# The opening of a graph network and Performer kernel rebuilt: one set of statistics for two normalisations

## What is computed

```python
def _layernorm(x, axis=-1, eps=1e-05):
    m = jnp.mean(x, axis=axis, keepdims=True)
    v = jnp.var(x, axis=axis, keepdims=True)
    return (x - m) / jnp.sqrt(v + eps)
...
    xn = _layernorm(x, axis=-1)
    x = x + _L0_gnn_ref(xn, edge_index, ...) + _L0_mix_ref(xn[None], ...)[0]
    x = x + _L0_ffn_ref(_layernorm(x, axis=-1)[None], ...)[0]
    return x
...
            for l in range(depth):
                h = _layernorm(x, ln1_s[l], ln1_b[l])
                q = heads(h @ Wq[l] + bq[l])
                k = heads(h @ Wk[l] + bk[l])
                v = heads(h @ Wv[l] + bv[l])
                qp = _softmax_kernel(q, proj[l], True)
                kp = _softmax_kernel(k, proj[l], False)
                attn = _linear_attention(qp, kp, v)
                x = x + (attn @ Wo[l] + bo[l])
```

## Time and profile before

| what | us |
|---|---|
| median of 3 runs | 1339.37 |
| lowest and highest of them | 1329.63, 1345.73 |
| profiled execution, its own time | 1338.45 |
| its span (first to last instruction) | 1336.6 |
| TensorE busy in it | 1186.8 (89%) |
| VectorE busy | 847.0 (63%) |
| ScalarE busy | 311.2 (23%) |
| GpSimd busy | 316.4 (24%) |

### The profile page before, as it was taken

How to read it: one execution, slowest core, us unless ns; L and a number is a source line. 1 busy time by engine, 2 the same in 40 slices (tenths; PEclk the granted TensorE clock), 3 DMA queues, 4 the chain that set the end, 5 groups by cost and what they waited for, 6 DMA issues and landing times.

```text
span 1336.6 us, 16673 instructions
## 1 busy us (share of the span) xinstructions
PE 1186.8 (89%) x5940; PEld 936.6 (70%) x5960; DVE 847.0 (63%) x1727; ACT 311.2 (23%) x584; POOL 316.4 (24%) x223
## 2 busy tenths in 40 slices
PE   1699979999999989887999999997888899899695
PEld 0577879888788877677998878884434588687432
DVE  7767447769953366764777995335787415616766
ACT  2234334423111003443442311100111112011212
POOL 4420200104733313020010563240000143300306
PEclk9899789999999989998999999999999999899897
DMA  6400100101312110000010131142000010101001
GB/s 197 157 1 1 32 1 1 32 1 48 111 32 64 36 56 1 0 31 2 1 33 1 53 105 42 54 185 78 1 1 0 9 32 32 32 1 30 1 0 63
DMA packets 15786, 52.12 MB, mean 39 GB/s; under 512 B 2624, under 2 KB 3456, under 8 KB 15200
## 3 DMA queue, kind: packets, MB, share of 16 engines
q1 hardware_dynamic: 11488, 39.18, 9.0%
q10 hardware_dynamic: 4224, 11.91, 2.5%
HBM read 44.80 MB, written 6.29 MB: 38 GB/s over the span
## 4 chain that ended last, share of the span: by engine, by line
PE 55%; DVE 23%; issue 15%; ACT 4%; POOL 2%; DMA 1%; SPq 0%; POOLq 0%; DVEq 0%; ACTq 0%
PE ps_a L401 6%; PE ps_v L401 6%; PE ps_a L403 6%; PE ps_a L402 6%; PE ps_v L402 6%; PE ps_v L403 6%; PE ps_v L556 5%; PE ps_a L658 4%; DVE f_hi L1157 4%; PE ps_v L762 2%; PE ps_v L569 2%; DVE f_lo L1159 2%; DVE expk L1269 2%; DVE ht_lo L1159 2%; PE ps_a L422 2%
## 5 line engine op out<-in xcount | busy, mean ns | idle before, releaser
L401 PE MATMUL ps_a<-ht_hi,w_hi 128*128 128x512 f32 x496 | 195.1, 393 | 2.4 <-DVE most_i L1429 2.4
L402 PE MATMUL ps_a<-ht_lo,w_hi 128*128 128x512 f32 x496 | 193.7, 391 | 0.0
L403 PE MATMUL ps_a<-ht_hi,w_lo 128*128 128x512 f32 x496 | 193.6, 390 | 0.0
L978 POOL TENSOR_TENSOR w_lo<-stage,w_hi 128x1024 fp32r<-128x1024 f32 x58 | 148.8, 2566 | 32.8 <-issue 28.5
L786 ACT ACTIVATE work<-ps_a,col_sb 128x512 f32<-128x512 f32 x96 | 66.4, 719 | 331.4 <-PE ps_a L403 207.7
L976 POOL CAST w_hi<-stage 128x1024 fp32r<-128x1024 f32 x58 | 67.9, 1171 | 242.4 <-PE ps_a L403 138.5
L1343 DVE TENSOR_TENSOR xm<-ps_v,xm 128x512 f32<-128x512 f32 x80 | 55.2, 690 | 94.4 <-PE ps_v L403 94.0
L401 PE MATMUL ps_v<-w_hi,ht_hi 128*128 128x512 f32 x224 | 94.5, 422 | 21.6 <-issue 8.8
L401 PEld LDWEIGHTS ps_a<-ht_hi,w_hi 128*128 128x128 f32 x496 | 93.5, 189 | 24.4 <-issue 2.6
L403 PEld LDWEIGHTS ps_a<-ht_hi,w_lo 128*128 128x128 f32 x496 | 93.5, 189 | 19.9
L402 PEld LDWEIGHTS ps_a<-ht_lo,w_hi 128*128 128x128 f32 x496 | 93.6, 189 | 19.5
(11 more groups left out here) (190 smaller groups left out, 2208.0 us busy)
## 6 DMA issues: line engine op xcount, KB each, us to landing
stage<-wstream SPq DMA_DIRECT2D x62, 512.0 KB, 3.6
nat<-x ACTq DMA_DIRECT2D x8, 256.0 KB, 6.4
xt_d<-xt_hi SPq DMA_DIRECT2D x1, 2048.0 KB, 6.3
xt_d<-xt_lo SPq DMA_DIRECT2D x1, 2048.0 KB, 10.8
ht_hi<-xt_d ACTq DMA_DIRECT2D x1, 2048.0 KB, 9.6
ht_lo<-xt_d ACTq DMA_DIRECT2D x1, 2048.0 KB, 15.4
x_again<-x ACTq DMA_DIRECT2D x8, 256.0 KB, 4.2
out<-xm SPq DMA_DIRECT2D x8, 256.0 KB, 2.0
```

The costliest lines, as they stand in the source:

```text
L401: nc.tensor.matmul(ps, left[0], right[0], start=first, stop=False)
L402: nc.tensor.matmul(ps, left[0], right[1], start=False, stop=False)
L403: return nc.tensor.matmul(ps, left[1], right[0], start=False, stop=last)
L978: nc.gpsimd.tensor_tensor(lo, stage[:, j, :], hi.bitcast(f32), ALU.subtract).then_inc(w_split, 1)
```

## The change

1. VectorE takes one set of statistics of x, by halves, and GpSimd makes both inverse deviations from it: `rstd` for the layer's normalisation (`first_deviation`) and `rstd_x`, `shift_x` for the residual.
2. x is loaded over two queues, even tiles on ScalarE's, odd ones on SyncE's, with a semaphore for each half; the identity goes in between, the edge ends and small constants behind the first weights.
3. VectorE normalises straight into `nat1`, half 0 before the statistics of half 1; ScalarE writes the residual `xm` later, after the first half's copies.
4. The first weights in the stream are V's. Their high part is made by ScalarE and their low part by VectorE. K's follow (ScalarE and GpSimd), then Q's (GpSimd).
5. The transposes of the residual and their split stand between V's tiles (after the fifth and the seventh), and x transposed is stored in three pieces from other places (`xt_hi` in slot 3, `xt_lo` in `nat`).
6. The block numbers, their maximum and the rounding of the head mask stand on VectorE behind V's last tile. TensorE waits for the mask ahead of K's product instead of at its start.
7. The output bias is added to the residual in attention's first eight `at` steps, in both layers, no longer behind each tile of V.
8. GpSimd's program is now: deviations, K's low weights (once half 0 of the input is split), Q's weights (once half 1 is), maximum over the partitions, bounds, and then the sums of V.

```diff
-HELPED = 2
+HELPED = 1
...
+XT_ORDER = [("xt", h, k) for h in range(H) for k in range(KT)]
+LATER_A = (
+    QK_ORDER
     + [("ddq", g, j) for g in range(STEPS) for j in range(2)]
     + [("o", h, k) for h in range(H) for k in range(KT)]
     + F0_ORDER
     + [block for c in range(1, FC) for block in by_halves(("f", c))]
 )
+
+A_JOBS = [numbered(N1_ORDER + (XT_ORDER if L == 0 else []) + LATER_A) for L in range(LAYERS)]
+A_OFF = [0, len(A_JOBS[0])]
...
-MIX_W = numbered(["q", "v", "k", "o"] + FFN_ORDER)
+W_NAMES = ["v", "k", "q", "o"] + FFN_ORDER
+MIX_W = numbered(["v", "k", "q", "o"] + FFN_ORDER)
+SLOT_OF = {"q": 0, "v": 1, "k": 2, "o": 3} | {name: n % SLOTS for n, name in enumerate(FFN_ORDER)}
...
+            for t in range(1, NT, 2):
+                sp.dma_start(nat[:, t, :], x[t * P:(t + 1) * P, :]).then_inc(x_in[t // 4], 16)
+                if t == 3:
+                    sp.dma_start(ident[:], ident_c).then_inc(ident_in, 16)
+            for j in range(PIECES):
+                sp.dma_start(stage[:, j, :], wstream[0, j]).then_inc(w_in[j], 16)
...
-            sp.wait_ge(a_empty, done(XT - 1))
-            for i in range(2):
-                sp.dma_start(xt_d[i], xt[i][:].bitcast(f32)).then_inc(xt_stored, 16)
+            sp.wait_ge(a_empty, done(A_JOBS[0][XT_ORDER[-1]]))
+            for n in range(2):
+                sp.dma_start(xt_d[0, :, 2 * n:2 * n + 2, :], xt_hi[n][:].bitcast(f32)).then_inc(xt_stored, 16)
+            sp.dma_start(xt_d[1], xt_lo[:].bitcast(f32)).then_inc(xt_stored, 16)
...
-            pe.wait_ge(consts_in, 96)
-
-            pe.wait_ge(mask_ready, 1)
-
-            for n in range(XT):
-                h, k = divmod(n, KT)
-                if k == 0:
-                    pe.wait_ge(x_normed, 4 * (h + 1))
-                turn(bank_a(n), [Xm[:, 4 * h + i, nodes(k)] for i in range(4)], a_full)
+            pe.wait_ge(ident_in, 16)
...
+                def turn_residual(h):
+                    pe.wait_ge(x_normed, 4 * (h + 1))
+                    for k in range(KT):
+                        turn(bank("a", ("xt", h, k)), [Xm[:, 4 * h + i, nodes(k)] for i in range(4)], a_full)
...
+                    if L == 0 and t in (4, 6):
+                        turn_residual(t // 2 - 2)
+                if L == 0:
+                    pe.wait_ge(mask_ready, 1)
...
-            for t in range(NT):
-                act.dma_start(nat[:, t, :], x[t * P:(t + 1) * P, :]).then_inc(x_in, 16)
+            for t in range(0, NT, 2):
+                act.dma_start(nat[:, t, :], x[t * P:(t + 1) * P, :]).then_inc(x_in[t // 4], 16)
+            act.dma_start(col_sb[:], cols[0]).then_inc(par_in, 16)
...
+            high_weight(0, SLOT_OF["v"])
+            load_parameters(0)
...
+                    if L == 0 and name == N1_ORDER[KT - 1]:
+                        high_weight(1, SLOT_OF["k"])
+                        act.wait_ge(rstd_x_ready, 1)
+                        for t in range(NT):
+                            nc.scalar.activation(Xm[:, t, :], nat[:, t, :], ACT.Identity, scale=rstd_x[:, t:t + 1],
+                                                 bias=shift_x[:, t:t + 1]).then_inc(x_normed, 1)
+                if L == 0:
+                    for name in XT_ORDER:
+                        _, h, k = name
+                        act.wait_ge(a_full, a0 + (MIX_A[name] + 1))
+                        nc.scalar.activation(xt_hi[k // 2][:, k % 2, half(h)], psA[:, MIX_A[name] % BANKS, :],
+                                             ACT.Copy).then_inc(xt_high, 1)
...
-            low_weight(0, 0)
-            both_halves(0, 0)
-            for s in range(1, HELPED):
-                low_weight(s, s)
-            both_halves(0, LN_FIRST)
+            def first_deviation(h):
+                columns = slice(4 * h, 4 * h + 4)
+                pool.wait_ge(var_ready, h + 1)
+                hold(pool)
+                nc.gpsimd.tensor_scalar(vare[:, columns], mv[:, columns, 1], 1.0 + EPS_LN, EPS_LN * EPS_LN, ALU.mult,
+                                        ALU.add).then_inc(eps_added, 1)
+                pool.wait_ge(eps_added, h + 1)
+                nc.gpsimd.tensor_tensor(rstd[:, columns], vare[:, columns], nhalf[:, columns], ALU.pow).then_inc(rstd_ready, 1)
+
+            first_deviation(0)
+            first_deviation(1)
+            nc.gpsimd.tensor_scalar(rstd_x[:], mv[:, 0:NT, 1], EPS_LN, None, ALU.add).then_inc(p_chain, 1)
+            pool.wait_ge(p_chain, 2)
+            nc.gpsimd.tensor_tensor(rstd_x[:], rstd_x[:], nhalf[:, 0:NT], ALU.pow).then_inc(p_chain, 1)
+            pool.wait_ge(p_chain, 3)
+            nc.gpsimd.tensor_tensor(shift_x[:], mv[:, 0:NT, 0], rstd_x[:], ALU.mult).then_inc(p_chain, 1)
+            pool.wait_ge(p_chain, 4)
+            nc.gpsimd.tensor_scalar(shift_x[:], shift_x[:], -1.0, None, ALU.mult).then_inc(rstd_x_ready, 1)
+            pool.wait_ge(split, done(MIX_SPLIT[N1_ORDER[KT - 1]]))
+            low_weight(1, SLOT_OF["k"])
+            pool.wait_ge(split, done(MIX_SPLIT[N1_ORDER[-1]]))
+            split_weight(2, SLOT_OF["q"])
...
-            pool.wait_ge(xt_stored, 32)
-            split_weight(2, 2)
+            pool.wait_ge(xt_stored, 48)
+
+            LATE_USERS = [(5, 6, 4), (4, 5, 6)]
...
-                for n in range(8, 15):
-                    kind, c = FFN_ORDER[n - 8]
+                for n, (kind, c) in zip(range(8, 15), [FFN_ORDER[i] for i in (0, 1, 2, 3, *LATE_USERS[L])]):
...
-            dve.wait_ge(ends_in, 32)
-            then(nc.vector.tensor_scalar(block_i[:], ends_i[:, 1, :], 7, None, ALU.arith_shift_right))
-            then(nc.vector.tensor_copy(block_f[:], block_i[:]))
-            for r in range(2):
+            def block_spans(r):
                 for b in range(NT):
                     last = nc.vector.scalar_tensor_tensor(out=spans[:, r, b, :], in0=block_f[:], scalar=float(b),
                                                           in1=group_no[:, r, :], op0=ALU.is_equal, op1=ALU.mult)
-            then(last)
-            nc.vector.tensor_reduce(span_p[:], spans[:], axis=AX.X, op=ALU.max).then_inc(span_ready, 1)
-            dve.wait_ge(consts_in, 96)
-            nc.vector.tensor_copy(headmask_r[:], headmask[:]).then_inc(mask_ready, 1)
-
-            dve.wait_ge(x_in, 16 * NT)
+                return last
+
             residual = lambda t: Xm[:, t, :]
-            normalise(lambda t: nat[:, t, :], Xm, x_normed)
-
-            dve.wait_ge(x_normed, NT)
-            deviations(residual, 0, LN_FIRST)
-
-            def split_input(h):
-                for k in range(KT):
-                    n = h * KT + k
-                    dve.wait_ge(xt_high, n + 1)
-                    nc.vector.tensor_tensor(xt[1][:, k, half(h)], psA[:, n % BANKS, :],
-                                            xt[0][:, k, half(h)].bitcast(f32), ALU.subtract).then_inc(a_empty, 1)
-
-            split_input(0)
-            normalise_half(residual, nat1, normed, 0, 0, LN_FIRST)
-            split_input(1)
+            loaded = lambda t: nat[:, t, :]
+
+            def low_weight(s, slot):
+
+                for j in range(PIECES):
+                    whole = slice(2 * j, 2 * j + 2)
+                    hi, lo = (w[:, slot, whole, :].rearrange("p a b -> p (a b)") for w in (Whi, Wlo))
+                    dve.wait_ge(w_high, s * PIECES + (j + 1))
+                    nc.vector.tensor_tensor(lo, stage[:, j, :], hi.bitcast(f32), ALU.subtract).then_inc(w_split, 1)
+
+            for h in range(H):
+                dve.wait_ge(x_in[h], 64)
+                statistics(loaded, half_tiles(h))
+                aggregate(half_tiles(h), h + 1)
+                if h == 0:
+                    normalise_half(loaded, nat1, normed, 0)
+            low_weight(0, SLOT_OF["v"])
...
+                def split_residual(h):
+                    for k in range(KT):
+                        dve.wait_ge(xt_high, h * KT + k + 1)
+                        nc.vector.tensor_tensor(xt_lo[:, k, half(h)], psA[:, MIX_A[("xt", h, k)] % BANKS, :],
+                                                xt_hi[k // 2][:, k % 2, half(h)].bitcast(f32), ALU.subtract).then_inc(a_empty, 1)
...
-                    nc.vector.tensor_tensor(Xm[:, t, :], Xm[:, t, :], rows_sb[:, 2, :], ALU.add)
                     if t == 2:
                         for k in range(KT):
                             split_t(("n1", 1, k), hT, k, 1)
+                    if L == 0 and t in (4, 6):
+                        split_residual(t // 2 - 2)
+                if L == 0:
+                    dve.wait_ge(ends_in, 32)
+                    then(nc.vector.tensor_scalar(block_i[:], ends_i[:, 1, :], 7, None, ALU.arith_shift_right))
+                    then(nc.vector.tensor_copy(block_f[:], block_i[:]))
+                    block_spans(0)
+                    then(block_spans(1))
+                    nc.vector.tensor_reduce(span_p[:], spans[:], axis=AX.X, op=ALU.max).then_inc(span_ready, 1)
+                    dve.wait_ge(consts_in, 80)
```

(5 more changed lines are left out.)

76 lines of the change are left out of this document (32 added, 44 removed).

## The result

| | before | after |
|---|---|---|
| median of the runs | 1342.02 us (4 runs, 1329.63 to 1345.73) | 1364.74 us (4 runs, 1357.32 to 1369.73) |
| ratio, 95% interval | | 1.0181 (1.0098 to 1.0264) |
| profiled execution, span | 1336.6 us | 1367.9 us |
| mean granted clock of TensorE, in shares of 2.4 GHz | 0.957 | 0.924 |
| the same kernels once more (run e14 below) | 1342.88 us (29 runs) | 1353.14 us (12 runs: eleven from 1335.19 to 1378.92, one of 1578.61) |

The forecast was 1336.0 us, range 1323 to 1344: wrong. The kernel became slower, by 1.8% in the first set of runs and by about 0.8% at the medians of the second (ratio 1.0054, interval 1.0011 to 1.0097).

A forecast was written before the change was run, and what follows sets the result against it. VectorE's chain in the opening, ahead of V's product, was taken to bound the kernel. 7.3 us gained, less 2.5 for sums and 3.0 for adds, plus 0.7, took 2.5 us off 1338.45: 1336.0 us, range 1323 to 1344.

The forecast's parts named there:

- x at 6.0 us: Opening: the first half of x, four loads over two queues, has landed at 6.0 us (bounds 4.4 and 8.4).
- Inverse deviation 1.4: Opening: the step from the variances to VectorE's first normalisation takes 1.4 us, besides any library load.
- V's low weights 2.8: Opening: VectorE makes V's low weights, two of 128x1024, in 2.8 us ahead of the splits.
- GpSimd's library, 7.3 us: Opening: GpSimd's code load, now behind the wait for the first variances, delays the normalisation 7.3 us (bounds 0 and 13.5).
- Rival B: Opening: GpSimd's library costs nothing at the start, 7.3 us better, 1328.7 us; chance 0.2.
- The mask's wait, 7.1 us: Ahead of K's product: TensorE waits for V's copy, 0.7 us, and the block work, 6.4 us.
- The slow clock behind it, 2.0 us: Behind the wait for the mask: TensorE's slow clock costs 2.0 us, leaving 7.3 us of the gain.
- The sums beside K's product, 2.5 us: K's product: GpSimd's seven sums of V now run beside it and cost 2.5 us (bounds 0 and 10.3).
- K's product by 66 to 76 us: Sign: K's product starts near 71 us; before 66 or after 76 us the prediction is wrong in the main.
- The adds in attention, 3.0 us: Attention, both layers: 16 output-bias adds of 0.68 us cost 3.0 us, about 1.5 a layer (bounds 0 and 10.9).
- Rival D: Attention is bound by VectorE, so the adds cost 10.9 instead of 3.0 us, 1343.9 us; chance 0.12.
- Rival E: K's product: the port lock makes GpSimd's sums cost 10.3 instead of 2.5 us, 1343.8 us; chance 0.08.

The follow-up runs named there:

- e14: The changed kernel once more, unedited, on another chip than its first runs: 1353.14 us.
- e7: The changed kernel with two adds ahead of each context-product wait, block numbers made between V's tiles and the head mask copied behind V's fourth: 1316.24 us, ratio 0.9830.
- e8: e7 with GpSimd's seven sums of V put ahead of the span and the bounds in layer 0: 1321.35 us, ratio 0.9838.

## Why the prediction was wrong

By its own steps:

- x at 6.0 us: 5.78. Statistics 3.0: 3.0. Inverse deviation 1.4: 1.9 from the aggregation's end to the normalisation. V's low weights 2.8: 2.3. Splits 4.3: 4.4. Right.
- GpSimd's library, 7.3 us: nothing. Its first arithmetic came 0.5 us behind the variances (8.78 to 9.31). Rival B. The rows 6.03 and 7.30 of the earlier trace rows stand beside library changes in the middle of the program, and no row showed one at the start; I gave the likelier place to the nearest row, where the bound of 0 was the case. At the change of library after the span, 9.93 us of "issue" stand again. The Trainium skill's 6 us for freshly loaded code (GPSIMD Engine Reference, "Instruction dispatch") does not show at the start.
- The mask's wait, 7.1 us: 7.2. The slow clock behind it, 2.0 us: K's product to the first square took 4.7 us against 3.0. Right, and by e7 worth undoing.
- The sums beside K's product, 2.5 us: the stage grew by 3.8 us (60.5 to 64.3). VectorE's part is in the groups of that stage, the changed kernel's first, with the mean ns of one behind the comma, then those of before:

```profile
L1280 DVE TENSOR_TENSOR sq_lo<-sq,sq_hi 128x512 fp32r<-128x512 f32 x15 | 12.4, 825 | 0.5
...
L1278 DVE CAST sq_hi<-sq 128x512 fp32r<-128x512 f32 x15 | 7.0, 464 | 14.3 <-ACT sq L871 14.2
```

```profile
L1237 DVE TENSOR_TENSOR sq_lo<-sq,sq_hi 128x512 fp32r<-128x512 f32 x15 | 10.4, 692 | 0.5
L1235 DVE CAST sq_hi<-sq 128x512 fp32r<-128x512 f32 x15 | 6.4, 426 | 10.1 <-ACT sq L846 10.0
```

That is 15 x 0.17 = 2.6 us. e8 takes 3 us back. Right in size.
- K's product by 66 to 76 us, else wrong in the main: it was at 59.9, 11.2 us early. 7.7 of them are the start of V's product, with the library. The rest is V's product itself, which ran 14.7 us from its fifth tile to its end where the forecast had 16.7: it carried over the 2.0 us of slow clock of the earlier trace rows, but with the wait of 6.2 us shrunk to 1.2 us the clock was full there (1.00 from 26.0 to 52.7 us). The opening with K's and Q's product gained 14.9 us where the sum had 4.8, and this unforeseen gain hid a part of the loss in attention.
- **The adds in attention, 3.0 us: this is the step that failed.** It priced an add by its own length and TensorE's wait by its own length, and put the clock at nothing. In its own terms it was of the right size: TensorE's idle time grew by 2.5 us in layer 0 and 2.7 us in layer 1, and taking from every profiled stage half of its slow stretches leaves 119.4 us on average for the 12 stages without an add in the steps and 121.6 us for the eight with all of them, a collision and no filling, so some 2 us a layer. What the sum lacked was the clock: 51 us of the changed kernel's attention in layer 0 and 68 us in layer 1 ran at 1.2 GHz, against 29 and 10 before, which costs half of the difference, 11 and 29 us of the 13.8 and 29.3. Not all of it is the collision's: in each layer 12 us are the stretch behind the eighth add, and in layer 1 another 7 are the one in the third context product and 10 the one at the stage's start, which kernels without the adds have in some executions too and which this execution had by chance. The upper bound of 10.9 us was no bound, since it too counted lengths.
- Rival D had the right place and the wrong mechanism: not 16 adds at 0.68 us, but above all one per layer that collides. Rival E had the right mechanism, GpSimd's lock, and looked for it beside the sums, not beside a weight's split in attention. The 2.76 us of the earlier trace rows was an event of that kind. The earlier trace rows took a window of 12 us without GpSimd (0.00), and so did not show it.

The slow stretches before were in the trace too, and a reader of the earlier trace rows, whose clock column says 1.00, could not know. One row of the stage's first 20 us in the kernel before (145.9 to 165.9 us) has 0.57:

```profile
145.90:165.90 20.00, 19.70 (x103) 19.38 (x102) 5.45 (x15) 0.18 (x1) 5.68 (x3) 0.57 0.18 53
```

By that stretch attention's time comes in two values, 124 to 126 and 133 to 134 us, in all 12 profiled stages without an add in the steps, and in either layer. I take it for most of the scatter of the kernel before, which has one profile, so this is not shown. What sets it stays open: the wait ahead of it is 1.8 us in both cases.
